# Layer 2 of a two-convolution kernel in blocks of 2 x 2 pixels, on even and odd column planes

## The reference

```
def _gn(v, G=16, eps=1e-05): ...      # normalise each image over groups of 2 channels
x = x + _L0_conv_ref(_gn(x), L0_conv_weight, L0_conv_bias)   # 9x9, zero padding, weights are
                                                             # Gaussians made from 3 parameters
x = x + _L1_conv_ref(_gn(x), L1_conv_weight)                 # 5x5, reflecting padding
```

## Time and profile before

| | us |
|---|---|
| median of 3 runs | 244.48 (244.34 to 244.93) |
| span of the profiled execution | 242.7 |
| PE busy (MATMUL) | 232.7, 1447 instructions |
| VectorE busy | 212.9, 463 instructions |
| ScalarE busy | 155.7, 333 instructions |
| POOL busy | 4.4, 12 instructions |

### The profile page before, as it was taken

One profiled execution on the slowest core, in us unless ns is written; L12 is line 12 of the kernel. 1 busy time (PEld: TensorE's weight loads), 2 busy tenths in 40 slices (PEclk: granted clock), 3 DMA queues, 4 the chain that ended last, 5 costly groups with the idle time before them and its releaser, 6 DMA issues.

```text
span 242.7 us, 4170 instructions
## 1 busy us (share of the span) xinstructions
PE 232.7 (96%) x1447; PEld 144.7 (60%) x1447; DVE 212.9 (88%) x463; ACT 155.7 (64%) x333; POOL 4.4 (2%) x12
## 2 busy tenths in 40 slices
PE   5699999899999999999999999999999999999995
PEld 5467666555566665555666665556666665655554
DVE  4989999699999999999989998999997359978943
ACT  5888898999399567999537592537358003569210
POOL 1000000050000000000000000000000000000000
DMA  6980022220015000003412000063020001521123
GB/s 207 379 332 4 6 72 54 69 64 0 3 41 167 7 1 0 0 3 101 136 75 97 0 4 0 12 185 115 1 100 0 0 0 46 163 101 55 48 97 97
DMA packets 8709, 17.24 MB, mean 71 GB/s; under 512 B 3312, under 2 KB 5616, under 8 KB 8688
## 3 DMA queue, kind: packets, MB, share of 16 engines
q1 hardware_dynamic: 7712, 16.64, 20.9%
q10 hardware_dynamic: 976, 0.34, 0.5%
HBM read 5.57 MB, written 4.72 MB: 42 GB/s over the span
## 4 chain that ended last, share of the span: by engine, by line
PE 71%; DVE 16%; ACT 6%; issue 3%; DMA 2%; ACTq 0%; DVEq 0%
PE banks L1425 34%; PE banks L1442 33%; DVE X L766 4%; PE banks L1389 3%; ACT junk L1059 3%; DVE lo L733 2%; DMA tab<-in_tables 2%; DVE whl L563 2%; PE banks L1501 1%; DVE work L558 1%; DVE s L703 1%; DVE partU L719 1%; ACT hi L1115 1%; PE banks L1375 1%; DVE s L706 1%
## 5 line engine op out<-in xcount | busy, mean ns | idle before, releaser
L1425 PE MATMUL banks<-hi,whl 128*128 128x360 f16 (+4 forms) x576 | 99.1, 320 | 1.4 <-ACT hi L1115 1.2
L1425 PEld LDWEIGHTS banks<-hi,whl 128*128 128x128 f16 x576 | 56.0, 99 | 35.7 <-issue 1.7
L1425 PE MATMUL banks<-lo,whl 128*128 128x376 f16 (+4 forms) x288 | 51.6, 320 | 0.5 <-DVE lo L733 0.5
L1059 ACT ACTIVATE junk<-X 128x576 bf16<-128x576 f32 x58 | 39.5, 681 | 2.1 <-DVE X L766 0.5
L1425 PEld LDWEIGHTS banks<-lo,whl 128*128 128x128 f16 x288 | 28.0, 98 | 17.9 <-DVE lo L733 1.1
L1442 PE MATMUL banks<-lo,wh 128*128 128x384 f16 (+1 forms) x165 | 31.8, 323 | 0.0
L1442 PE MATMUL banks<-hi,wh 128*128 128x384 f16 (+1 forms) x165 | 31.8, 323 | 0.0
L1442 PE MATMUL banks<-hi,wl 128*128 128x384 f16 (+1 forms) x165 | 31.8, 323 | 0.0
L1115 ACT CAST hi<-work 128x416 f16<-128x416 f32 x32 | 16.6, 536 | 19.9 <-PE banks L1442 14.1
L1115 ACT CAST hi<-s 128x384 f16<-128x384 f32 x32 | 15.3, 508 | 17.9 <-DVE s L700 12.2
L1105 ACT ACTIVATE work<-work,gof,gsc 128x26 f32<-128x26 f32 (+1 forms) x48 | 23.3, 576 | 3.6 <-DVE gof L644 3.6
(11 more groups left out here) (138 smaller groups left out, 231.7 us busy)
## 6 DMA issues: line engine op xcount, KB each, us to landing
X<-in_x SPq DMA_DIRECT2D x8, 576.0 KB, 9.6
out<-X SPq DMA_DIRECT2D x7, 576.0 KB, 3.0
work<-X SPq DMA_DIRECT2D x8, 432.0 KB, 3.8
whl<-work SPq DMA_DIRECT2D x24, 64.0 KB, 2.0
work<-X SPq DMA_DIRECT2D x8, 144.0 KB, 3.6
stage<-in_w SPq DMA_DIRECT2D x1, 640.0 KB, 7.6
work<-X SPq DMA_DIRECT2D x32, 12.0 KB, 2.3
out<-X SPq DMA_DIRECT2D x1, 384.0 KB, 2.6
```

The lines of the kernel that those rows point to most:

```text
L1059: nc.scalar.activation(waste, image(n, m), function, accum_out=sums[c][:, col:col + 1]).then_inc(sums_done[c], 1)
L1425: ins = nc.tensor.matmul(dst[:, :, o0:o1], w[1][:, i, t * P:(t + 1) * P], src[:, :, o0 + dx:o1 + dx], start=(first and part == 0 and t == ...
```

## The change

**Layout.** X, the input and the output keep even and odd columns in separate planes (`PLANE`, `HW` = 24 columns). A layer-1 matmul whose column tap is odd, 4 of 9, reads the other plane and is issued as two matmuls of about 192 columns.

**Layer 2.** For layer 2 the shift regroups the partitions: 2 rows x 2 columns x 32 channels, so a matmul contracts a block of 2 x 2 pixels. The 5 x 5 kernel becomes 3 x 3 taps of such blocks. The row transform now makes 6 streams for 4 outputs, 3 taps each: a pair takes 6 streams x 3 parts x 3 taps = 54 matmuls of 288 columns, where it took 60 of 384. `streams2` is 7 operations (2 on a larger part of P2, then 5), `out2(n)` stands for 4 PSUM steps, 4 row steps and 2 end steps.

**Low halves.** VectorE no longer makes layer 2's low halves. `high_two` (ScalarE) casts two streams at once to f16 (`hi`) and writes them a second time as f16, negated (`lo`); then `lows2` has POOL issue a transfer that adds the float32 streams to `lo`, which leaves the rest. TensorE waits for its landing (`lo2_landed`) ahead of the third part of each stream. A pair has three such groups. `hi` and `lo` of layer 2 are double buffered now, `P2` is single.

**Residual and store.** The result of layer 2 is built in a buffer `u2`, and X is not added by VectorE: once layer 1 of a quad is through, `prefill` (SP, 4 transfers a pair) writes X to the output, and `store` (POOL) adds `u2` to it there.

**Shift.** 14 transfers a pair instead of 6, since each column plane goes to its own partitions, and the 8 prefill transfers of a quad stand between its two shifts. SP has 146 rows of instructions where it had 46.

**Order.** TensorE: quad 0, quad 1, pair 0, pair 1, quad 2, pair 2, quad 3, pairs 3 to 7, with the banks dealt out oldest first: pair 0 takes 3, 2, 4, 1, 0, 5, pair 1 takes 6, 3, 2, 4, 1, 0, and quad 2 begins with 5. The hand-written lists of VectorE and ScalarE are rewritten from quad 1 on.

```diff
-M1, M2 = 6, 3
-TILES1, TILES2 = T // M1, T // M2
+M1, M2 = 6, 4
+TILES1, TILES2 = T // M1, (H // 2) // M2
...
+PE_ORDER = (("quad", 0), ("quad", 1), ("pair", 0), ("pair", 1), ("quad", 2), ("pair", 2), ("quad", 3),
+            ("pair", 3), ("pair", 4), ("pair", 5), ("pair", 6), ("pair", 7))
...
+STATS_AFTER = {("quad", 1, 4): (2, 0), ("quad", 1, 6): (1, 2), ("quad", 2, 0): (1, 3), ("quad", 2, 2): (2, 1),
+               ("quad", 3, 0): (2, 2), ("pair", 4, 2): (2, 3)}
...
+                for q in range(2):
+                    src = pair(n)[:, (1 - q) * PLANE:(2 - q) * PLANE]
+                    at, p0 = 1 - q, 2 * q * C
+                    body, far = at + U2 * ROW, at + T * ROW
+                    sp.dma_start(zf[p0:p0 + 2 * C, body:body + PLANE], src[C:3 * C, :]).then_inc(done, 16)
...
+            def prefill(n):
...
+                        sp.dma_start(dram_pair(out, n)[2 * q * C:2 * (q + 1) * C, a * PLANE:(a + 1) * PLANE],
+                                     pair(n)[2 * a * C:2 * (a + 1) * C, q * PLANE:(q + 1) * PLANE]).then_inc(prefilled[n], 16)
...
             for qd in range(NQ):
                 shift(2 * qd)
+                prefill(2 * qd)
+                prefill(2 * qd + 1)
                 shift(2 * qd + 1)
...
+                stt(alpha2.rearrange("p h (u y) -> p h u y", y=ROW2), rows_of_two(P2, 1), -4.0, rows_of_two(P2, 2),
+                    ALU.mult, ALU.add).then_inc(parts2_done, 1)
...
+                tt(delta2, halves[:, :, ROW2:U2 * ROW2], halves[:, :, 0:T * ROW2], ALU.subtract).then_inc(parts2_done, 1)
...
+                tt(s32_2[:, 0, :], alpha2[:, 0, :], alpha2[:, 1, :], ALU.add).then_inc(s_done[2], 1)
...
+            def rows2(n):
...
+                wait(dve, stored[n % 2], 16 * (n // 2))
...
+            def out2(n):
+                middle2(n, 0)
+                middle2(n, 1)
+                rows2(n)
+                end2(n, 4)
+                end2(n, 5)
...
+                out2(3)
+                streams2(5)
                 small_stats(2, NQ - 1)
...
+                streams2(6)
+                out2(4)
+                streams2(7)
+                out2(5)
+                out2(6)
+                out2(7)
...
+                act.wait_ge(s_done[2], 5 * n + (2, 4, 5)[g])
+                wait(act, conv_mm[2], NS2 * (n - 2) + 2 * g + 2)
+                nc.scalar.copy(hi[2][:, b, at, :], s32_2[:, at, :]).then_inc(hi_done[2], 1)
+                nc.scalar.mul(lo[2][:, b, at, :], s32_2[:, at, :], -1.0).then_inc(negative_done, 1)
...
+                    pool.dma_start(lo[2][:, b, at, :], s32_2[:, at, :], accum_op=ALU.add).then_inc(lo2_landed[g], 16)
...
+                pool.wait_ge(prefilled[n], 64)
+                pool.wait_ge(out_done[2], 6 * (n + 1))
+                pool.dma_start(dram_pair(out, n), u2[n % 2], accum_op=ALU.add).then_inc(stored[n % 2], 16)
...
+            READ2 = {0: lambda n: (m_read[2], 2 * n + 1), 1: lambda n: (mid_done[2], 4 * n + 2),
+                     2: lambda n: (m_read[2], 2 * n + 2), 3: lambda n: (mid_done[2], 4 * n + 4),
+                     4: lambda n: (out_done[2], 6 * n + 5), 5: lambda n: (out_done[2], 6 * n + 6)}
```

More of the change, by code:

```diff
@@ L979, in fourth_quad @@
                 streams1_ends(3)
-                low_halves(1, 3, range(2, 4))
-                middle2(3)
-                rows2(3)
+                low_halves(3, range(2, 4))
+                out2(2)
                 streams1_wide(3)
-                low_halves(1, 3, range(4, 8))
-                end2(3, 2)
-                end2(3, 3)
+                low_halves(3, range(4, 8))
+            def fourth_quad():
+                streams2(3)
                 small_stats(2, 2)
@@ L1121, in read_m1, with highs2 @@
+            def highs2(n):
+                for g in range(3):
+                    high_two(n, g)
             def read_m1(qd, g):
@@ L1422, in conv1 @@
                         dx = t - PAD1
[L1423 to L1427 removed]
+                        weights = w[1][:, i, t * P:(t + 1) * P]
@@ new lines, in conv1 @@
+                        begins, ends = first and part == 0 and t == taps[0], last and part == 2 and t == taps[-1]
+                        if dx % 2 == 0:
+                            o0, o1 = max(0, -dx // 2), HW - max(0, dx // 2)
+                            src = xbuf[1][:, i, :].rearrange("p (r x) -> p r x", x=HW)
+                            ins = nc.tensor.matmul(dst.rearrange("p h q r x -> p (h q r) x")[:, :, o0:o1], weights,
+                                                   src[:, :, o0 + dx // 2:o1 + dx // 2], start=begins, stop=ends)
+                        else:
+                            src = by_plane1(xbuf[1][:, i, :])
+                            for q in range(2):
+                                e = (dx + q - (1 - q)) // 2
+                                o0, o1 = max(0, -e), HW - max(0, e)
+                                ins = nc.tensor.matmul(dst[:, :, q, :, o0:o1], weights, src[:, :, 1 - q, :, o0 + e:o1 + e],
+                                                       start=False, stop=ends and q == 1)
@@ L1435, in conv2 @@
                     if part == 0:
[L1436 to L1443 removed]
+                        pe.wait_ge(hi_done[2], 3 * n + g + 1)
@@ L1444, in conv2 @@
+                    if part == 2:
+                        pe.wait_ge(lo2_landed[g], 16 * (n + 1))
+                    src = xbuf[2][:, b, k, :].rearrange("p (r x) -> p r x", x=HW2)
+                    for a in range(B2):
+                        ins = nc.tensor.matmul(dst, wbuf[2][:, k, a * P:(a + 1) * P], src[:, :, a:a + HW],
+                                               start=(part == 0 and a == 0), stop=(part == 2 and a == B2 - 1))
                 ins.then_inc(conv_mm[2], 1)
```

660 lines of the change are left out of this document (318 added, 342 removed).

## The result

The changed kernel takes **281.22 us** (median of 4 runs, 281.02 to 282.28), the kernel before 244.5 us beside it. The ratio is 1.151, with a 95% interval of 1.149 to 1.153. The profiled execution took 281.02 us with a span of 278.9, so 2.1 us lie around the span. The forecast was 268 within 250 to 282: the sign and the range hold, the range by 0.8 us, and the point is 13 us low.

The account below looks back on a forecast made before the run. TensorE was taken to bound the second half, but in-order waits to outweigh its 23.7 us gain. Last row step 214.4, VectorE's end 261, store 5: span 266, plus 1.8 around it, 268 us; range 250 to 282.

Parts of the forecast that it names:

- The walk: Seven steps following the engines' fixed orders from VectorE's step at 79.75 to the end: 268 us, itself 262 to 272; 40%.
- Steps 1 to 5: Front to last row step: VectorE waits for ScalarE, quad 2 begins 17 us late, TensorE idles 5.3, R at 214.4.
- 0 to 10%: Possible extra cost in streams2 from VectorE reading every second row, up to 2 us behind R.
- Step 6: Tail after R: pair 7's copy arrives at R + 26.4 = 240.8, its matmuls end at 260, end2 at 261.
- rival (c): Adding transfers are slow, passing through one queue in order with stores between: 268 + 12 = 280; chance 15%.
- Rival (d): TensorE's clock halves after waits: last pair 13.4 instead of 6.7 us, quad 3 some 2 more; 276; chance 25%.
- Step 7: Last store at the end: issue and an adding 576 KB transfer, taken as 5 us; span 266.
- (a): Throughout, the waits hardly arise because VectorE runs nearly full: 235 us; chance 5%.
- (b): Half of the waits: quad 2 begins 8 us late instead of 17, tail 4 shorter; 250 to 256; chance 15%.
- (e): Layer matmuls save less than claimed, since half-size ones cost more than 84 ns; chance below 3%.

Follow-up runs that it names:

- the single moves: One edit each to the changed kernel: last quad's shifts ahead of prefills, 271.1 us; normalise1(2) ahead of pair 1's groups, 276.2; quad 2's statistics one stream later, 277.85.
- the rearranged kernel: The changed kernel with all three single moves, plus ScalarE's and VectorE's orders around pairs 0 and 1 rearranged to empty PSUM banks earlier: 260.45 us.
- three moves: All three single moves together on the changed kernel (shifts ahead of prefills, normalise1(2) ahead of casts, statistics one stream later): 261.97 us.
- The best version found: The rearranged kernel with its tail reordered too, half of pair 6's copy on GpSimd's queue and pair 7's low halves by VectorE: 257.6 us.

## Why the prediction was right, and where 13 us were missing

The walk against the trace, times in us:

```
                                             forecast   measured
streams2(0)                                  89.5-93.9  89.8-94.2
streams2(1)                                 102.2-106.5 101.8-106.2
streams1_near(2) begins                        114.1      113.1
middle2(0,0), which empties bank 2             121.8      120.8
quad 2 begins                                  129.5      128.4
statistics matmul of quad 3                    180.2      178.7
last row step ends (R)                         214.4      214.8
pair 7's copy is there                         240.8      247.8
streams2(7) ends                               247.6      254.9
pair 7's matmuls end                           260        269.8
VectorE ends                                   261        271.0
span                                           266        278.9
```

**Steps 1 to 5 held.** Up to R the walk is never off by more than 1.5 us, and that most at the statistics matmul. The 0.4 us at R are in part luck: what was early there was lost again to the half clock in quad 3 (1.7 us), which the walk left out. The price of a 288-column matmul (124 ns, measured 126) and of streams2 (4.4, measured 4.4, so no row shows the "0 to 10%" for reads of every second row) are those of the forecast, a group on ScalarE is shorter (1.23 us for 1.35), and the waits stand in their places (VectorE 5.9 us where 6.6 was forecast, the statistics matmul 4.3 where it was 5.3). Two of the single moves show that these waits are causes: 5.0 and 3.4 us come back when the one instruction is moved that each was blamed on.

**Step 6, the copy: 7.0 us short.** The step that failed is "z_loaded for pair 7 is R + 26.4". It is R + 33.1 (6.7 more; the rest of the 7.0 is R's lateness). By its terms: the first list took 9.2 us (9.8 forecast), the prefills 8.6 (4.5), the second list 11.3 (9.8), the landing 4.0 (2.3). With the low-half transfers gone the whole is 25.1, 1.3 less than forecast. I had asked of those transfers only how long they last themselves (3 us forecast; median 3.8, in the tail up to 7.2). What they do is slow the queue beside them: 5.2 us on SP's issues, 2.7 on the landing. This is rival (c) in its size (12 us forecast, 9.0 measured) by another mechanism. Two edits each take this away, the shifts first (10.1) and the low halves by VectorE (9.0); they touch the same wait and were not run together alone.

**Step 6, the clock: 2.6 us.** The walk had 1.00 all through. Rival (d) was right that it falls, and where: behind waits of 3 to 6 us, in pairs 0 and 1, in quad 3 (1.7 us where (d) had 2), in pairs 5 and 6. It was wrong on the price of the last pair, 6.7 us more: pair 7 itself ran at full clock (18 groups at 0.38 us, 6.8 us), since the clock was up again at 261.5 and pair 7 began at 263.0; only the part of pair 6 from 255.87 on counts. And this is no separate fault: in the three kernels whose copy comes some 8 us sooner (shifts first, plain stores, low halves on VectorE) pair 6 runs at full clock from its third stream on, with no matmul added. The late copy makes TensorE wait 6.2 us, and the half clock follows. In front of quad 2 the slow matmuls lie between bank waits; that they cost nothing there was not tested.

**Step 7, the store: 2.9 us.** "I take 5" from the end of VectorE's work to the end; it is 7.9 (271.0 to 278.9). With plain stores the same stretch is 5.0 (260.4 to 265.4), so the adding is the whole of it. It lies inside the bounds I gave (4.6 more than the 5). The Trainium skill's estimate for such a transfer (DMA: Bandwidth & Descriptors, Anatomy of one DMA — SWDGE: about 2 us plus bytes at 436 GB/s, so 3.4) fits the plain store of 3.3 and not the adding one of 6.0; the measurement decides.

7.0 + 2.6 + 2.9, with 0.3 more around the span (2.1 instead of 1.8) and 0.2 between the profiled execution and the median, is 13.0 of the 13.2 us. So the waits were foreseen and the tail was mis-sized. The walk's own bounds, 262 to 272, miss the result; the range holds by 0.8 us only because it reached up to (c), and both (c) and (d) came with other mechanisms or prices than stated. That part is luck.

**The other rivals.** (a) held that VectorE runs nearly full. The amount was right (148), the conclusion falls with the time itself: VectorE stands idle for 51 of the 199 us behind 79.75. Two runs say the same of the amount: 10.4 us more VectorE work ahead of R left it where it was, and 6.7 us more in the rearranged kernel cost 1.4. (b) had quad 2 begin 8 us late; it was 16.1. (e) falls with the 126 ns.

**Where the 25 us of TensorE went.** With front and three moves mended the last row step ends at 204.6, as in the kernel before (204.11): up to there the change then costs and gains the same. Behind it the tail takes 52.7 us instead of 38.6. Of these 14.1 us, 5.8 lie behind VectorE's last step: 8.0 us to the end, where it was 2.2. The other 8.3 lie before it, where VectorE is busy 38.0 us instead of 28.9 and TensorE 31.8 instead of 35.9: TensorE has less to do and nothing comes of it. How much of the 8.3 is VectorE's work and how much the copy with its 14 pieces instead of 6 was not measured. The best version found, 257.6, is 5% behind the kernel before. Shifts first together with all low halves on VectorE, on top of the rearranged front, was not tried.

## What to carry to other kernels

Walk the fixed orders of the engines step by step and the waits come out within some 1.5 us; but price each DMA queue with the others running, since a transfer that is hidden itself can delay the one that is waited for. In the tail, look at what stands ahead of the last needed copy in its queue: eight transfers that nobody waited for cost 10 us of 281, and moving them is one line. And a sum of busy time says little about what an engine can still take: 10 us more on VectorE moved the last row step by 0.2 us.

## What the runs showed of the hardware

- A store of 576 KB from GpSimd's queue lands in 3.3 us plain and in 6.0 us when it adds to memory (5.7 to 7.5); its issue holds GpSimd 0.56 and 0.87 us. The adding low-half transfers (128x624, float32 to float16 within SBUF) land in 3.1 to 7.2 us, 3.8 in the median.
- SP issues one transfer each 0.64 us. Beside GpSimd's transfers single issues stretch to 1.2 to 1.9 us, to 1.75 also beside a plain store; eight prefills took 8.5 us beside the low-half transfers and 5.1 without them.
- With the stores adding, GpSimd's queue took 22.3% of the DMA engines' time of 278.9 us, with plain stores 17.4% of 265.4, for the same 8.55 MB; with adding stores and no low-half transfers 10.6% of 270.3 for 4.72 MB. From these three, as an estimate, 1 MB takes the 16 engines 8.8 us as an adding transfer within SBUF, 6.1 as an adding store and 2.7 as a plain one.
- TensorE's matmuls of 288 columns start every 126 ns at full clock and every 240 ns at half. The half clock (granted clock 0.50) was there after waits of 2.9 to 6.2 us. Behind the waits of 2.9 and 4.3 us the first matmuls still ran at full speed and the clock fell 0.4 and 0.8 us later. Added matmuls in the place of the waits kept it at full speed.
